# Weight quantisation ahead of the feed-forward stage: 24 chunks moved in front of it, and a third queue for the chunk loads

## What is computed

```python
x = layernorm(x + attn(x))     # latent attention, 16 heads, causal, scores clipped to +-80
x = layernorm(x + ffn(x))
# ffn: both weights are fake-quantised, each with one scale for the whole matrix
scale = max(abs(W)) / 127
Wq = clip(round(W / scale), -128, 127) * scale
h = gelu(x @ Wq_fc.T + b_fc + 2 * (x @ A_fc.T) @ B_fc.T)      # W_fc 4096 x 1024
y = h @ Wq_proj.T + b_proj + 2 * (h @ A_proj.T) @ B_proj.T    # W_proj 1024 x 4096
```

## Time and profile before

| | |
|---|---|
| time before, median of 2 runs | 2221.25 us (2219.2 to 2223.29) |
| the profiled execution | 2219.89 us |
| span of its slowest core (core 4), which all rows here show | 2218.3 us |
| spans of the 8 cores | 2206.7 to 2218.3 us |
| mean granted TensorE clock of the 8 cores | 0.760 to 0.765 |

### The profile page before, as it was taken

One profiled execution on the slowest core, in us unless ns is written; L12 is line 12 of the kernel. 1 busy time (PEld: TensorE's weight loads), 2 busy tenths in 40 slices (PEclk: granted clock), 3 DMA queues, 4 the chain that ended last, 5 costly groups with the idle time before them and its releaser, 6 DMA issues.

```text
span 2218.3 us, 28219 instructions; the slowest of 8 cores (2206.7 to 2218.3 us)
## 1 busy us (share of the span) xinstructions
PE 1343.3 (61%) x7038; PEld 680.4 (31%) x7038; DVE 1018.0 (46%) x1317; ACT 881.8 (40%) x1229; POOL 83.5 (4%) x136
## 2 busy tenths in 40 slices
PE   0073776667677675344542333316889889898895
PEld 0020122222222222011100111104557566575664
DVE  2257677777777778634547544441120101201012
ACT  0000366666666665133450155552332323323231
POOL 0000000000000000000000000000000000000000
PEclk9585988878878878577655655558989899898997
DMA  5500012221221214222110122230000000000000
GB/s 187 133 33 0 10 60 66 66 65 43 65 65 63 65 49 137 96 80 76 57 53 0 30 85 83 82 93 15 20 18 4 20 1 20 20 1 20 1 20 20
DMA packets 49662, 112.29 MB, mean 51 GB/s; under 512 B 12528, under 2 KB 23280, under 8 KB 47200
## 3 DMA queue, kind: packets, MB, share of 16 engines
q0 software_dynamic: 14912, 54.53, 7.6%
q1 hardware_dynamic: 23936, 32.60, 4.9%
q10 hardware_dynamic: 10656, 23.34, 3.6%
HBM read 97.47 MB, written 8.39 MB: 48 GB/s over the span
## 4 chain that ended last, share of the span: by engine, by line
PE 38%; DVE 23%; ACT 17%; DMA 12%; issue 8%; ACTq 1%; DVEq 1%; SPq 0%; POOLq 0%
PE PSD L313 31%; DVE CL L681 6%; ACT PT L688 4%; ACT QSG L788 4%; DMA QSG<-wFCr 4%; DMA QSG<-wPRr 4%; DVE MXW L554 3%; PE BIG L597 3%; PE PSD L665 2%; DVE CL L674 2%; ACT QTI L792 2%; DMA STG<-xT 1%; ACT TSQ L1166 1%; ACT HH L1114 1%; DVE XT L1036 1%
## 5 line engine op out<-in xcount | busy, mean ns | idle before, releaser
L688 ACT ACTIVATE PT<-CL 128x1024 bf16<-128x1024 f16 (+1 forms) x320 | 310.8, 971 | 183.8 <-DVE CL L674 97.1
L313 PE MATMUL PSD<-XT,RTF 128*128 128x256 bf16 x2048 | 306.0, 299 | 123.4 <-ACT HH L1114 121.5
L681 DVE TENSOR_SCALAR CL<-PSD 128x1024 f16<-128x1024 f32 x192 | 235.2, 1225 | 73.3 <-PE BIG L597 30.8
L313 PE MATMUL PSD<-HH,RTP 128*128 128x256 bf16 x2048 | 236.1, 274 | 52.3 <-DVE UPt L1131 52.3
L665 PE MATMUL PSD<-QH,KH 96*128 96x512 bf16 (+3 forms) x640 | 198.9, 403 | 112.5 <-DVE CL L674 51.2
L313 PEld LDWEIGHTS PSD<-XT,RTF 128*128 128x128 bf16 x2048 | 194.8, 105 | 196.4 <-issue 140.6
L597 PE MATMUL BIG<-PT,VP 128*65 128x512 bf16 (+3 forms) x640 | 197.8, 397 | 66.9 <-ACT PT L688 54.7
L313 PEld LDWEIGHTS PSD<-HH,RTP 128*128 128x128 bf16 x2048 | 196.0, 98 | 83.7 <-issue 54.4
L1114 ACT ACTIVATE HH<-PSD,BFCS,SML 128x256 bf16<-128x256 f32 x256 | 144.3, 564 | 142.1 <-PE PSD L313 125.9
L788 ACT ACTIVATE QSG<-QSG,SML 128x512 f32<-128x512 f32 x128 | 104.0, 813 | 217.3 <-DMA QSG<-wFCr 80.8
L801 DVE TENSOR_TENSOR QSG<-QSG,QTI 128x512 f32<-128x512 f32 x128 | 88.6, 693 | 124.0 <-ACT QTI L792 118.8
(11 more groups left out here) (148 smaller groups left out, 1337.6 us busy)
## 6 DMA issues: line engine op xcount, KB each, us to landing
STG<-wFCr POOLq DMA_DIRECT2D x32, 512.0 KB, 4.5
STG<-wPRr POOLq DMA_DIRECT2D x32, 512.0 KB, 4.5
STG<-xT SPq DMA_DIRECT2D x8, 1024.0 KB, 6.2
QSG<-wFCr POOLq DMA_DIRECT2D x32, 256.0 KB, 3.0
QSG<-wFCr ACTq DMA_DIRECT2D x32, 256.0 KB, 2.8
QSG<-wPRr POOLq DMA_DIRECT2D x32, 256.0 KB, 3.1
QSG<-wPRr ACTq DMA_DIRECT2D x32, 256.0 KB, 2.7
out<-OST SPq DMA_DIRECT2D x64, 128.0 KB, 1.9
```

The lines of the kernel that those rows point to most:

```text
L313: e.matmul(outap, la, ra, start=st, stop=sp),
L681: e.tensor_scalar(self.CLB[cs][:, 0:qw], self.PSD[pslot][:, 0:qw], 80.0, -80.0, ALU.min, ALU.max),
L688: etok = P.s(lambda e, cs=cs, qw=qw: e.activation(self.PTB[cs][:, 0:qw], self.CLB[cs][:, 0:qw], AF.Exp, scale=ISQ), waits=[ctok, self.pv_t ...
```

## The change

1. At the end of phase 4, behind the 64 apply instructions, there are 24 calls of `emit_quant_chunk`. They make the fronts of the next 24 chunks (48 to 71: the last 16 of W_fc, the first 8 of W_proj). `q_rtp_free` is set ahead of them. 56 chunks are left for t = 0.
2. From chunk count 32 on, the loads go over three queues in turn: POOL where the count is divisible by 3, ACT at remainder 1, SP at remainder 2. Each queue has semaphores of its own; below 32 the queues are as before.
3. The wait for the end of attention stands on the first four chunk loads instead of the first two.
4. The ten low-rank loads wait for the user of the buffer two counts before them instead of three (the later of the two).
5. M2R, a row of 256 bf16 used in the second layer norm, is placed at the high end of SBUF.

```diff
-        self.M2R = A.alloc("M2R", [1, TC], BF16, 7, 7)
+        self.M2R = A.alloc("M2R", [1, TC], BF16, 7, 7, side="high")
@@ _quant_front
-        if c < 2:
+        if c < 4:
             w_dma += self.q_rt_free + self.attn_evac_last
-        ld = P.d("scalar" if c % 2 else "gpsimd", "dqw",
+        qq, qs = ((("gpsimd", "dqw"), ("scalar", "dqs"))[c % 2] if c < 32
+                  else (("gpsimd", "dqw"), ("scalar", "dqs"),
+                        ("sync", "dqy"))[c % 3])
+        ld = P.d(qq, qs,
                  lambda e, qsg=qsg, src_ap=src_ap: e.dma_start(
                      qsg[:, 0:512], src_ap),
                  waits=w_dma)
@@ phase4, its last lines
         self.ph4_bar = [self.xt_rdy[7], rt, sq_last, self.absmax_last]
+        self.q_rtp_free = list(self.xt_rdy.values()) + [self.wo_done]
+        for _ in range(24):
+            self.emit_quant_chunk()
@@ phase5, the low-rank loads
-                waits=[self.q_prev.get(("p4", self.qn - 4))] + xt_all + bar)
+                waits=[self.q_prev.get(("p4", self.qn - 3))] + xt_all + bar)
```

## The result

The changed kernel takes 2198.25 us (median of 11 runs) against 2220.83 us (median of 10) for the kernel before, run beside it: a ratio of 0.9908, 95% interval 0.9884 to 0.9932. The medians are 23 us apart, against 22 forecast; the ratio puts the gain at 20 us, 15 to 26. It is inside 2%. Runs of both kernels now and then take 1 to 2% longer with one half of the chip at a lower clock; the ratios here leave those out, the medians don't.

A forecast was written before the change was run, and what follows sets the result against it. Chunks, slowed by ACT waiting behind loads in its own queue, were taken as the bound. Terms -4.0 + 57.8 + 4.6 - 80.4 = -22.0 us took 2219.9 to 2197.9, stated as 2199 for the median; 80% range 2184 to 2220.

The forecast's parts named there:

- What bounds it: W_fc at t = 0: no engine full, chunks set the pace; ACT idles 69.2 us for chunk loads before p1.
- B: As a stretch: first Gelu to PE's restart on W_proj, forecast 167.3 us instead of 247.7, -80.4.
- rival A: Chunk loads: the third queue brings nothing, as loads await freed buffers and share transfer engines; +11.0, 2231 us; chance 0.14.
- The schedule of t = 0: 28 blocks with two chunks each at 5.5 us instead of 6.27, then four bare blocks and the APT product: -80.4 us.
- (1,2), (0,1) and (2,0): Blocks of t = 0, named by their two chunks' counts modulo 3 (0 POOL, 1 ACT, 2 SP): 6.27, 6.21, 3.87 us.
- rival B: Phase 4 and t = 0: an ACT load doesn't start under a Gelu or square; +8, 2207 us; chance 0.2.
- The sums of phase 4: Squares of phase 4: ACT loads hide under squares in five of seven periods, 53.6 us against 56.5, 1.1 less behind: -4.0.
- The 24 chunks: Between last XT and last p4: moved chunks at 2.45 us each with PE idle, +57.8 us.
- Rival C: Apply stage of phase 4: the 24 chunks find cover beneath it; -57.8 more, 2140 us; chance 0.04.
- The split by edit: The whole change divided: the move alone (24 calls, low-rank loads) +11.0 us, the third queue -33.0.
- A: As a stretch: end of last XT to first Gelu (moved chunks, low-rank loads, low-rank product), forecast +62.4 us.
- Nothing lost later: t = 1 to 7 and W_proj keep their work; PE at most enters W_proj warmer, 0 to -1.5 us.

The follow-up runs named there:

- the first pair: The changed kernel, and the same without the 24 calls at the end of phase 4, each first measured against the kernel before: ratios 0.9908 and 0.9868.

## Why the prediction was right

**What bounds it** held: the chunks set the pace of t = 0 and ACT's wait behind the load in its own queue set that of the chunks. That was only argued from the rows; the run without ACT loads shows it, with 60 us out of B at the same number of queues. A row of the kernel before fits it. The load issued at 1359.03 fills the buffer of the chunk three before, and this is that chunk's p4:

```profile
1354.12 0.69 DVE L809 TENSOR_TENSOR RTP<-QTI,QSG 128x512 bf16<-128x512 int8 x1 [0.31 <-DVE QSG L801]
```

It ends at 1354.81. So the buffer was free for 4.2 us while the load stood in ACT's queue. This also answers rival A's reason, that a load can't be issued before its buffer is free: here the queue, and not the buffer, held it.

**The schedule of t = 0** held to 1 us on the profiled core (-79.6 for -80.4) and came out 2 us shorter than forecast on the mean of the cores (165.5 against 167.3). Blocks of 6.3, 6.2 and 3.9 us were forecast for (1,2), (0,1) and (2,0); over the nine triples they measure 6.6, 6.25 and 3.9. Three of the nine (1,2) blocks make the difference: they took 6.9, 7.2 and 7.8 us, with waits of 3.1, 3.4 and 4.0 us for ACT's load, where the other (1,2) blocks wait 2.4 to 2.6; why those loads took longer was not tried. An ACT load does start beneath a Gelu (1340.05), and beneath a square, as these rows of the changed kernel show, so rival B is out:

```profile
1100.60 1.91 ACT L970 ACTIVATE YC<-YC 128x2048 bf16<-128x2048 bf16 x1 [2.46 <-PE PSD L965]
1100.73 0.34 ACTq L788 DMA_DIRECT2D QSG<-wFCr  x1
```

**The sums of phase 4** came to -4.2 for -4.0 by two misses that cancel: the squares gained 3.7 and not 2.9, as the two periods with a load behind p2 took 7.50 and 7.76 us and not 8.07, and behind the last square it was 0.5 and not 1.1.

**The 24 chunks** cost +60.2 instead of +57.8. Three chunks took 7.6 us instead of 7.35 on the mean (ACT issues a load at 1238.06 and, 21 chunks on, at 1291.47: 53.41 / 7). The first three took 8.2, the later ones 7.2 to 7.9; why the first are slower was not tried. Rival C, cover beneath the apply stage, is out by the row at 1237.93: p2 of chunk 48 waits 67.02 us for the QTI that p4 of chunk 46 frees behind the last XT, so only one p1 found cover. Whether calls placed between the apply instructions would find cover was not tried.

**The split by edit** was +11.0 for the move with the low-rank wait and -33.0 for the queues. Measured: +9.2 for the kernel with the first two alone. From there to the changed kernel the medians, of different chips, give 2198.3 - 2230.9 = -32.6, and the ratios, 0.9908 - 1.0039, give -29. By the stretches the first part is +9.5: 4.7 for the low-rank wait (A of the kernel without the calls against before) and 4.8 for the calls themselves.

**Rival A**, for which the Trainium skill's rule (Trainium Kernel Development and Optimization, Key Constraints) spoke, is out by the queues alone (-29 us) and by the run with POOL and SP. No run here tests the rule's first half, that the transfers share engines: DMA was busy 0.30 of the stretch. The runs show what its second half, "only saves the sequencer's issue time", leaves out, that a load in the queue of a computing engine stands behind that engine's own work, and its consumer right behind it.

**Nothing lost later:** from PE's restart to the end it is 706.6 us, before 707.4.

**The total** owes something to luck. By the mean of the cores A gave +64.4 for +62.4 and B -80.9 for -80.4; with -4.2 for the sums of phase 4 that is -20.7, and the ratio says -20.4. The 22.6 us between the medians lie nearer to the forecast than its terms do. The first four waits, M2R's place and the separate semaphores stood at nothing; no run separates them from the rest.

The prediction didn't ask what else was to be had: with no loads on ACT and without the 24 calls, 63 us against the kernel before; with a fourth buffer, another 26.

## What to carry to other kernels

Don't issue a load from the queue of the engine that consumes it, right ahead of its use: the latency (here 2.8 us) then stands bare each time. An idle queue such as SP's or POOL's can wait for the buffer by itself. Work beneath which PE already runs should not be moved ahead of it for another engine's idle time alone: here ACT's idle time hid one p1, because two later steps of each chunk (p3 and p4) stood behind 64 apply instructions in DVE's list. And a wait written one step too tight ("two before" for "three before") costs time, here 4 to 6 us over ten small loads, and shows in no count of instructions.

## What was not expected

The prediction held only loads and steps that were there already; it did not see that one more buffer of 2 KB per partition would take the wait for loads away almost wholly. In the kernel with four buffers the p1 of its 50 chunks in the QSG buffers wait 6.0 us together, and the blocks came out at 3.88 us, the very sum of ACT's steps. Loads from POOL and SP then run at 128 GB/s, with the DMA engines busy 0.43 of the stretch, and their latency of about 3 us is still hidden. The place for the buffer was to be had in a tile that is not written before the blocks end.

The repeated runs were a surprise too: 0.987 was expected for the queues alone and 0.9894 came out, above the changed kernel's 0.9885, while the stretches showed 6.6 us, where the first pair had shown 7.7. A difference this small has to be read from the stretches.
